# Turnings of maxima, values, first input and first residual tiles placed behind the value products in a Flamingo block on one Trainium2 core

## What is computed

```python
x = x + tanh(g_xattn[0]) * xattn(layernorm(x), ctx_2048, Wq, Wk, Wv, Wsk, Wsv, Wo)
x = x + tanh(g_ffn[0]) * ffn(layernorm(x), ...)
# xattn: q from [ctx, x] (32 heads of 16), keys and values from x and from ctx (8 heads),
# scores / 4 + alibi bias, masked to a window of 64 later positions, softmax over both, times values, times Wo
# ffn: router softmax, top 4 of 128 experts, 8 basis products silu(x Wg) * (x Wu) mixed per token,
# a down product, plus a shared silu expert
```

## Time and profile before

| | us |
|---|---|
| median of 3 runs | 871.36 |
| the profiled execution, its own time | 872.62 |
| its span (first to last instruction) | 870.6 |
| PE busy | 858.4 (99%) |
| DVE / POOL / ACT busy | 545.2 / 519.9 / 399.3 |

### The profile page before, as it was taken

How to read it: one execution, slowest core, us unless ns; L and a number is a source line. 1 busy time by engine, 2 the same in 40 slices (tenths; PEclk the granted TensorE clock), 3 DMA queues, 4 the chain that set the end, 5 groups by cost and what they waited for, 6 DMA issues and landing times.

```text
span 870.6 us, 17391 instructions
## 1 busy us (share of the span) xinstructions
PE 858.4 (99%) x6662; PEld 753.4 (87%) x6662; DVE 545.2 (63%) x984; ACT 399.3 (46%) x807; POOL 519.9 (60%) x532
## 2 busy tenths in 40 slices
PE   9899999999999999999999999999999999999998
PEld 8889999999999998988888877888888888888886
DVE  7675666766666657756446756556655655665567
ACT  5754545554545544655035243444444444444431
POOL 3861443535335232343769998548888887888641
PEclk9999999999999999999999999999999999999999
DMA  8678676776868659630101354320212022021046
GB/s 275 170 143 180 152 207 186 191 196 167 205 165 218 163 139 256 144 100 25 49 25 49 102 168 157 134 73 25 82 40 73 25 72 73 25 84 38 1 151 236
DMA packets 76509, 108.09 MB, mean 124 GB/s; under 512 B 7274, under 2 KB 47979, under 8 KB 75403
## 3 DMA queue, kind: packets, MB, share of 16 engines
q1 hardware_dynamic: 74168, 105.94, 43.4%
q10 hardware_dynamic: 2258, 1.03, 0.5%
HBM read 70.71 MB, written 31.00 MB: 117 GB/s over the span
## 4 chain that ended last, share of the span: by engine, by line
PE 84%; POOL 10%; DMA 2%; DVE 2%; issue 1%; SPq 1%; ACT 0%; POOLq 0%; ACTq 0%
PE ps_scores L2227 20%; PE ps_proj L1846 15%; PE ps_scoresT L2227 10%; PE ps_scoresT L1983 7%; PE ps_o L1997 6%; PE ps_scores L1956 5%; PE ps_proj L2227 5%; PE ps_proj L1904 5%; PE ps_scores L1846 3%; PE ps_proj L1835 3%; PE ps_scoresT L1846 1%; DMA q_stack<-max_rows 1%; POOL sum_lo L953 1%; POOL sum_raw L968 1%; POOL sum_raw L966 1%; DMA xn_rows<-in_x 1%
## 5 line engine op out<-in xcount | busy, mean ns | idle before, releaser
L1128 ACT ACTIVATE probsT<-ps_scoresT 128x512 f32<-128x512 f32 (+1 forms) x256 | 138.9, 545 | 148.9 <-PE ps_scoresT L1983 144.4
L1490 DVE TENSOR_REDUCE neg_max<-ps_scores 128x2 f32<-128x384 f32 (+1 forms) x256 | 131.6, 516 | 108.6 <-PE ps_scores L1956 107.8
L1357 ACT ACTIVATE part_sums<-ps_scores 128x512 f32<-128x512 f32 x96 | 57.4, 598 | 130.1 <-PE ps_scores L2227 130.0
L1983 PE MATMUL ps_scoresT<-q_stack,k_stack 116*128 116x256 f32 x448 | 106.1, 307 | 0.8 <-DMA q_stack<-max_rows 0.8
L841 POOL TENSOR_TENSOR o_normal<-o_blocks,inv_sums 128x256 f32<-128x256 f32 x32 | 19.9, 622 | 138.0 <-DVE inv_sums L1511 138.0
L1956 PE MATMUL ps_scores<-k_stack,q_stack 114*128 114x192 f32 (+1 forms) x512 | 94.5, 267 | 2.7 <-DMA q_stack<-qT_hi 1.6
L1956 PEld LDWEIGHTS ps_scores<-k_stack,q_stack 114*128 114x128 f32 x512 | 83.0, 190 | 9.5 <-DMA q_stack<-qT_hi 2.3
L996 POOL TENSOR_TENSOR w_expert_lo<-w_sums,w_expert_hi 128x256 fp32r<-128x256 f32 x64 | 64.2, 1014 | 44.9 <-ACT w_expert_hi L1277 44.9
L1008 POOL TENSOR_TENSOR big<-big,basis 128x512 f32<-128x512 f32 x56 | 77.9, 1409 | 16.3 <-DVE basis L1785 16.3
L1983 PEld LDWEIGHTS ps_scoresT<-q_stack,k_stack 116*128 116x128 f32 x448 | 70.8, 190 | 4.7 <-DMA q_stack<-max_rows 1.0
L1776 DVE TENSOR_TENSOR basis<-part_sums,silu_gate 128x512 f32<-128x512 f32 x32 | 24.2, 755 | 67.3 <-ACT silu_gate L1365 67.3
(11 more groups left out here) (309 smaller groups left out, 2500.9 us busy)
## 6 DMA issues: line engine op xcount, KB each, us to landing
k_stack<-k_kept SPq DMA_DIRECT2D x64, 192.0 KB, 4.3
big<-coeff_rows SPq DMA_DIRECT2D x8, 1024.0 KB, 4.8
q_stack<-q_kept SPq DMA_DIRECT2D x40, 192.0 KB, 4.1
q_kept<-qT_hi SPq DMA_DIRECT2D x10, 512.0 KB
x_rows<-in_x SPq DMA_DIRECT2D x9, 512.0 KB, 5.8
k_kept<-kT_hi SPq DMA_DIRECT2D x16, 256.0 KB
x_kept<-x_rows SPq DMA_DIRECT2D x16, 256.0 KB, 2.6
w_raw<-in_L_ffn_w_gate SPq DMA_DIRECT2D x16, 256.0 KB, 2.8
```

The costliest lines, as they stand in the source:

```text
L1128: act.activation(PT[:, g % 2, 2 * j:2 * j + blocks].rearrange("p h f r w -> p (h f r w)"), ST[:, n % 2, 0:blocks].rearrange("p h n -> p (h ...
L1357: act.activation(TP[:, u % 2, j, :], src[:, u % 2, :], ACT.Copy).then_inc(taken, 1)
L1490: dve.tensor_reduce(NM[:, g // 2 % 2, g % 2, 2 * i:2 * i + 2], SA[:, n % 2, :, 0:keys], AX.X, ALU.max, negate=True).then_inc(max_done, 1)
L1983: ins = pe.matmul(ST[:, n % 2, v, :], KS[0:ROWS, g, j + v, 1 - v].rearrange("p w s -> p (w s)"), QS[0:ROWS, g, j + v].rearrange("p f r w - ...
```

## The change

It moves steps between slots and inside a slot; no instruction is added or removed, and none changes its shape.

- `NM_TURN` goes from 9 to 10 (`PAIR + 2`): the maxima are turned in the slot of the value products, right behind them, instead of in the slot before. `STACK_MAX`, the DMA of the rows, goes from slot 8p + 10 to 8p + 11.
- `TURN_V` goes from 19 to 18, `PREP` from (-41, -37) to (-38, -36), the first residual tile from slot 73 to 74, those of batch 4 (`SPILLED`) from (87, 91) to (90, 94).
- `scores_turned` stands behind `prep`, `turn_v` and `turn_x` in a slot instead of ahead of them.
- The wait of `turn_max` on the exponentials is rewritten so that it asks for the same number as before.

```diff
-MAX_HALVES, NM_TURN, STACK_MAX = PAIR, PAIR + 1, PAIR + 2
+MAX_HALVES, NM_TURN, STACK_MAX = PAIR, PAIR + 2, PAIR + 3
-PREP, K_PROJ, V_PROJ = (-41, -37), (-33, -32, -31), (-12, -11, -10)
+PREP, K_PROJ, V_PROJ = (-38, -36), (-33, -32, -31), (-12, -11, -10)
-TURN_V, TIMES_WO, LAST_WO = 19, ((56, 57, 59), (60, 61, 62)), ((56,), (59,))
+TURN_V, TIMES_WO, LAST_WO = 18, ((56, 57, 59), (60, 61, 62)), ((56,), (59,))
 def x_turn_slot(b, t):
-    return (62, 63)[t] if b == B - 1 else (87, 91)[t] if b == SPILLED else (73, 77)[t]
+    return (62, 63)[t] if b == B - 1 else (90, 94)[t] if b == SPILLED else (74, 77)[t]
...
             unit = PAIR * p + NM_TURN - LAG
             pe.wait_ge(nm_lo, p + 1)
-            if unit >= 2:
-                pe.wait_ge(exp_done, unit - 1)
+            if unit >= 3:
+                pe.wait_ge(exp_done, unit - 2)
...
             if p is not None:
                 turn_max(p)
-            if LAG <= n < END + LAG:
-                scores_turned(n - LAG)
             for t in range(TB):
                 b = due(n, PREP[t], 2)
...
                     turn_x(b, t)
+            if LAG <= n < END + LAG:
+                scores_turned(n - LAG)
             if n < PIECES:
                 queries(1, 1, n, PIECES)
```

## The result

Four runs of the changed kernel gave a median of 901.56 us (900.21 to 902.59), beside 871.06 (870.62 to 877.08) for the kernel before on the same chip: a ratio of 1.034 with a 95% interval of 1.032 to 1.036, so slower by 30 us. The forecast was 898.2. The profiled execution took 900.21 against 872.62, 27.6 more, where the sum said 26.8.

The account below looks back on a forecast made before the run. TensorE (PE), busy 858.4 of 870.6 us, was taken as the bound, so its pauses count one for one. Terms 25.0 + 2.5 - 1.2 - 0.8 + 0.9 + 0.4 = 26.8 gave 898.2 us, range 893 to 903 (8 in 10: 891 to 904).

Parts of the forecast that it names:

- The new wait: The odd unit's turned scores wait for ACT's copy of the maxima, behind the exponentials: 30 x 0.80 + 1.0 = 25.0 us.
- The restart: A pair of turned scores takes 0.50 behind a wait, 0.42 in the stream: 31 x 0.08 = 2.5 us.
- The turning in its new place: Turning the maxima behind the value products partly hides in the slow start there: -1.2 us, bounds -2.5 and +5.0.
- the end of the small matmuls, paid again: Worst case for the maxima's turning behind value products: slow start and small matmuls' end again, 31 x 0.16 = +5.0 us.
- The other turnings at 0: Some 20 other turnings put behind the value products keep their number and work, so 0 us.
- Input tiles: First input tiles, two slots apart, share a bank; the second waits for DVE: +0.9 us over 6 batches, bounds 0 and 5.
- The waits that go: PE's waits on DVE at the turning of the maxima vanish, since DVE has a slot more: -0.8 us.
- The late DMA of the maxima: The DMA is issued one slot later; the one late case of 32 gets later: +0.4 us, bounds 0 and 2.
- the clock falls: Rival: pauses drop the granted clock from 2.4 to 1.2 GHz behind each, 50 us on top, 948 us; 2 in 100.
- The pause does not arise: Rival: no pause at the 31 exits from the value products, and the new place saves: 865.6 us; 3 in 100.
- Half won back: Rival: the pause exists, but early waits on DVE or savings from other turnings win half back: 888 us; 6 in 100.
- More late than the odd unit: Rival: second input tile and DMA at upper bounds, 904 us, or 910 with the turning's upper bound; 14 in 100.

Follow-up runs that it names:

- kernels 1 and 2: Kernel 1 has its own line; kernel 2 is the changed kernel with a second ACT copy of the maxima ahead of the real one: 905.57 us, ratio 1.040.
- kernel 1: The kernel before with only the turning of the maxima (slot 10) and its DMA (slot 11) moved: 898.24 us, ratio 1.031.
- experiment 6: Two variants of kernel 1: the maxima copied out by DVE (878.38 us), or by ACT ahead of the exponentials (877.65 us); both ratio 1.007.
- Kernel 8: The kernel before with the maxima turned between the two halves of the value products and ACT's copy ahead of the exponentials: 879.26 us, ratio 1.008.
- kernel 4: The changed kernel with the turning of the maxima and its DMA back in their old slots, other turnings left in new places: 882.31 us, ratio 1.012.
- kernel 3: The changed kernel with ACT's copy of the maxima ahead of the exponentials of the same slot: 882.46 us, ratio 1.013.
- kernel 6 with DVE's copy: Kernel 1 with the turned maxima copied out by DVE instead of ACT: 878.38 us, ratio 1.007.
- kernel 7: The changed kernel with the turned scores ahead of the other turnings in a slot, as before; tables stay changed: 893.62 us, ratio 1.024.

## Why the prediction held, step by step

**What bounds the kernel.** Held. PE's list sets the time, and a pause on it counts one for one (kernels 1 and 2).

**The new wait.** The mechanism, the place and the count held; the size was 10% low. The term was 30 x 0.80 + 1.0 = 25.0. Measured by starts it is 0.885 each and 1.15 for the last pair (1.73 from the four matmuls' start to the next product instead of 0.58): 27.7. The step that was short is "an end on DVE let PE start 0.06 on", taken over to ACT's copy: behind the copy it is 0.14. That is all of the 0.08.

The reason is neither the engine nor the size of the copy but the form of the wait. The odd unit has two waits, and PE's records show the one on the copy (`nm_out`) as an instruction of its own ahead of the weight load, while the load carries the other (`exp_done`, written first in the code). Only unit 1, the odd unit of pair 1, has the wait on `nm_out` alone, and there the load carries it. Kernel 1 has both cases, with the same copy, at pairs 1 and 3:

```profile
51.82 0.25 ACT L1114 ACTIVATE max_rows<-ps_scoresT 32x128 fp32r<-32x128 f32 x1
52.12 0.30 PEld L1983 LDWEIGHTS ps_scoresT<-q_stack,k_stack 116*128 116x128 f32 x2 [0.80 <-ACT max_rows L1114]
52.13 0.51 PE L1983 MATMUL ps_scoresT<-q_stack,k_stack 116*128 116x256 f32 x2 [0.63 <-ACT max_rows L1114]
```

```profile
73.11 0.25 ACT L1114 ACTIVATE max_rows<-ps_scoresT 32x128 fp32r<-32x128 f32 x1
...
73.47 0.30 PEld L1983 LDWEIGHTS ps_scoresT<-q_stack,k_stack 116*128 116x128 f32 x2 [0.86 <-ACT probsT L1128]
73.50 0.48 PE L1983 MATMUL ps_scoresT<-q_stack,k_stack 116*128 116x256 f32 x2 [0.72 <-ACT max_rows L1114]
```

From the copy's end to PE it is 0.05 at the first (52.07 to 52.13) and 0.14 at the second (73.36 to 73.50). The trace of before has the same pair of cases behind DVE's copy of a tile (L1455): 17.72 to 17.87 where the wait stands by itself, 30.56 to 30.62 where the load carries it. With the wait on the load the pause would be about 0.80, as forecast, and the trip of experiment 6 about 0.09 shorter. That is an estimate: no run writes the two waits the other way round.

**The restart.** Held in kind, too high: 0.05 a pair, 31 x 0.05 = 1.5 instead of 2.5. In the changed kernel the weights of the waiting pair start at 161.39 and its matmuls at 161.42:

```profile
161.39 0.30 PEld L1983 LDWEIGHTS ps_scoresT<-q_stack,k_stack 116*128 116x128 f32 x2 [0.86 <-ACT probsT L1128]
```

So the load runs 0.03 ahead of its matmul, in the stream 0.09. In the earlier trace rows and at pair 1 above, where the load itself carried the wait, the two start together, and the restart is the dearer one. The rule of the Trainium skill, TensorE: Matmul & The Clock Gate, section "Step-by-step: what each phase is for", that the queue pulls weight loads ahead of matmuls in flight, gives no free restart here: the load does not pass the wait.

**The turning in its new place.** Right in sign. Where it stands alone behind the value products (kernel 1), the even unit starts 0.04 after it and takes 0.32 to 0.33 instead of 0.34, so it costs some 0.02 and saves 0.08 to 0.09 in the slot it left: -0.06. Where four other transposes follow, in 20 of 31 slots, it takes 0.12 and the even unit 0.32, which is +0.10 against -0.09. Together -0.4, forecast -1.2. Kernel 8 shows that "the end of the small matmuls, paid again" was a real case, only for another place.

**The other turnings at 0.** This step was wrong in its reason. I wrote that they keep their number and their work. They do, but each had covered something where it stood, and without the pause their new places cost 11 us in kernel 4 and some 9 in kernel 3. Beside the pause only a part shows: the changed kernel is 3.3 us above kernel 1 by medians, and its batch takes 50.27 us (107.60 to 157.87) where kernel 1 takes 50.07, 0.20 more instead of the 1.25 of kernel 4. Since the forecast was for both together, the number came out right by help of a cover that I had not named. That part was luck.

**Input tiles.** +0.9 with an upper bound of 5. With the pause there, one wait of 0.7. Without it, 5.4: the upper bound, "DVE one stream turn late", is what happens when DVE gets no time to catch up.

**The waits that go.** Those at L1971 went (-0.8). The late DMA of the maxima, forecast +0.4, went too (-0.8 and its restart). No kernel of this study lists it among its first waits, not even those with the maxima in the old place; I did not find out why.

Sum by measured terms on the profiled executions: 27.7 + 1.5 - 0.4 - 0.8 + 0.7 - 0.9 = 27.8, and -1.0 behind the last value products; some 27 of the 27.6 found. The -1.0 is not the change's: four of the twelve traces have it (this one and those of kernel 3, of kernel 6 with DVE's copy and of kernel 7); in the others that stretch is within 0.32 of the kernel before. The sum leaves out that the scores waited 1.3 more for DVE and 0.7 less for a DMA, and the turned scores once 0.6 for DVE. The median stands 1.35 above the profiled execution here and stood 1.3 below it before, which makes most of the distance from 898.2 to 901.56. Two of the four runs had spans of 900.2 and 900.6 with a mean granted clock of 0.997 and 0.996, two 898.1 and 898.3 near 1.0. So a small part of the rival "the clock falls" is in the median.

**The rivals.** "The pause does not arise": refuted by kernels 1 to 3. "Half won back": of the 10.8 us that it took off, the turnings give 0.4. "More late than the odd unit" named the tiles' wait with its right size, but it shows only where the pause is absent. "The clock falls": not behind these pauses of 0.88 us in the profiled execution, whose mean granted clock is 1.00; it did fall behind a wait of 1.67 us in kernel 4.

## What to carry to other kernels

Count a trip from PE through another engine and back by its starts, from the producing matmul to the consumer (0.73 to 0.75 us here, even on an idle engine), and put at least that much independent work between; what another engine has in its list ahead of the copy comes on top. Look also which of two waits the weight load carries: here the one that ended last stood by itself and cost 0.09 more. A step that seems free to move may be the cover of its neighbours: look at what stands just behind its old place, and price that without it. When a change brings one large pause, smaller waits hide in it, so what is left after mending the pause must be measured and not subtracted.

## What the runs showed of the hardware

- From an end on ACT, DVE or POOL to the start of the matmul that waited for it: 0.05 to 0.06 us where the weight load carries that wait (191 cases in the twelve traces), 0.14 to 0.15 where the wait is an instruction of its own ahead of the load (157 of 162; for the other five the profile names an end 0.00 to 0.04 before the start). The size of the operation makes no difference: the copy of 32 x 128 and DVE's copy of 128 x 512 show both numbers.
- A turning with 128 columns of moving data amid matmuls with 32 columns of weights takes 0.215 between them and makes 0.35 in all; behind the last of them 0.04.
- The granted clock fell to 1.2 GHz for 3.4 us behind a wait of 1.67 us; PE had been busy for 1.18 of the 2 us before. The pauses of 0.88 us, one to a pair and some 12 us apart, left it at 2.4 GHz in the profiled execution.
- A copy of 32 x 128 out of PSUM takes 0.25 to 0.27 us on ACT and 0.28 on DVE.
